# A memory layer on one NeuronCore: recall turned and values weighed as 32-row tiles, one per batch and head

## The reference, cut to what matters

```python
def step(carry, inp):                       # per batch b and head h, 32 tokens
    mem, z = carry                          # 64 x 64 and 64
    q_s, k_s, v_s, qn_s, kn_s = inp
    scores = einsum('bhnd,bhmd->bhnm', q_s, k_s) * SCALE      # rotated q, k
    sdpa = einsum('bhnm,bhmd->bhnd', softmax(where(mask, scores, -inf)), v_s)
    sq = elu1(qn_s)
    num = einsum('bhnk,bhkv->bhnv', sq, mem)
    den = einsum('bhnk,bhk->bhn', sq, z)[..., None]
    out = beta * num / (den + 1e-06) + (1.0 - beta) * sdpa
    sk = elu1(kn_s)
    prev_v = einsum('bhnk,bhkv->bhnv', sk, mem) / einsum('bhnk,bhk->bhn', sk, z)[..., None]
    mem = mem + einsum('bhnk,bhnv->bhkv', sk, v_s - prev_v)
    z = z + sk.sum(axis=2)
    return ((mem, z), out)
```

## Time and profile before

| | |
|---|---|
| median of 3 runs | 2612.66 us (2610.97 to 2617.28) |
| span of the profiled execution | 2623.8 us; no other time of this execution is given |
| memory layer in it | about 1729 to 2452 us |
| rounds with scores | 128, from 1760.2 to 2434.1 |
| `spread` on GpSimd | 128 x 1273 ns, 162.9 us |
| `weigh`'s first part (L2104) on TensorE | 512 records, 79.2 us |
| `weigh`'s second part (L2107) on TensorE | 1024 records, 85.5 us |
| granted TensorE clock | 1.00 from 1780 to 2425 (2.4 GHz), 0.72 on average from 1750 to 1780, 0.80 from 2425 to 2450 |
| busy from 2000 to 2100 | TensorE 94.4, VectorE 91.3, ScalarE 71.7, GpSimd 72.0 of 100 us |

### The profile page before, as it was taken

The page is one execution under the profiler, slowest core; times in us unless marked ns, Lnnn a source line. Parts: engine busy times, 40 slices in busy tenths (PEclk is TensorE's granted clock), DMA queues, the critical chain, the costliest instruction groups (busy, mean ns, idle before and its releaser), DMA issues. The chain is left out here.

```text
span 2623.8 us, 79243 instructions
## 1 busy us (share of the span) xinstructions
PE 2176.9 (83%) x30448; PEld 1549.2 (59%) x30448; DVE 1700.0 (65%) x5819; ACT 1437.8 (55%) x3704; POOL 1106.7 (42%) x1076
## 2 busy tenths in 40 slices
PE   6499948589964889899999977948999999999696
PEld 3288845379862233333334336937778777787396
DVE  6722247642336778787878833358999989899522
ACT  5455544355552256455455555537777767776353
POOL 2066644146654120120200004547777777776164
PEclk7699979789986799998989888969999999999798
DMA  4011120011125121111111000121111111111013
GB/s 133 33 42 43 43 85 2 33 32 44 43 93 163 55 58 31 38 39 31 35 46 35 5 33 29 41 85 54 54 53 56 52 53 55 52 56 52 35 42 92
DMA packets 76025, 134.96 MB, mean 51 GB/s; under 512 B 17225, under 2 KB 32264, under 8 KB 73224
## 3 DMA queue, kind: packets, MB, share of 16 engines
q1 hardware_dynamic: 62080, 102.07, 12.6%
q0 software_dynamic: 13568, 27.81, 3.7%
q10 hardware_dynamic: 8, 0.00, 0.0%
HBM read 65.19 MB, written 32.79 MB: 37 GB/s over the span
## 5 line engine op out<-in xcount | busy, mean ns | idle before, releaser
L1544 ACT ACTIVATE ca_pt<-ca_ps 128x512 f32<-128x512 f32 (+3 forms) x768 | 341.1, 491 | 322.3 <-PE ca_ps L1649 137.2
L734 PE MATMUL ffn_ps<-ffn_xst,ffn_up_w 128*128 128x128 f32 x3392 | 420.8, 278 | 0.2 <-issue 0.2
L734 PEld LDWEIGHTS ffn_ps<-ffn_xst,ffn_up_w 128*128 128x128 f32 x3392 | 402.9, 195 | 1.2 <-issue 1.2
L857 DVE TENSOR_TENSOR ffn_hid<-ffn_sg,ffn_ps 128x512 f32<-128x512 f32 x212 | 145.8, 688 | 359.2 <-PE ffn_ps L734 110.9
L576 POOL DMA_INDIRECT ffn_xs<-ffn_x,ffn_token_at x212 | 205.2, 968 | 301.5 <-DVE ffn_token_at L840 165.5
L581 POOL DMA_INDIRECT ffn_y<-ffn_ys,ffn_result_at x212 | 208.8, 985 | 139.2 <-DVE ffn_ys L863 82.3
L1645 PE MATMUL ca_ps<-ca_stacks 75*128 75x512 bf16 (+3 forms) x768 | 245.2, 342 | 18.3 <-ACT ca_pt L1544 10.7
L1777 DVE TENSOR_REDUCE ca_m_far<-ca_ps 128x1 f32<-128x128 f32 (+5 forms) x384 | 236.7, 616 | 30.3 <-PE ca_ps L1623 27.9
L643 ACT ACTIVATE ffn_sg<-ffn_ps 128x512 f32<-128x512 f32 x212 | 125.7, 593 | 233.6 <-remote 182.3
L1623 PE MATMUL ca_ps<-ca_stacks 72*128 72x512 bf16 (+3 forms) x768 | 223.4, 356 | 34.1 <-DVE ca_m_near L1778 21.9
L1778 DVE CUSTOM_DVE_ANT_0 ca_spill<-ca_ps,ca_bias_q 128x256 f32<-128x256 f32 (+1 forms) x512 | 201.1, 397 | 10.9 <-PE ca_ps L1623 10.9
(11 more groups left out here) (340 smaller groups left out, 4742.0 us busy)
## 6 DMA issues: line engine op xcount, KB each, us to landing
im_mates<-im_t SPq DMA_DIRECT2D x256, 128.0 KB
ffn_got<-ffn_y SPq DMA_DIRECT2D x48, 256.0 KB, 5.8
ca_stacks<-scratch_q_piece SPq DMA_DIRECT2D x16, 576.0 KB
ca_stacks<-scratch_k_piece SPq DMA_DIRECT2D x48, 192.0 KB
ffn_x<-ffn_xn SPq DMA_DIRECT2D x32, 256.0 KB, 2.0
w_w<-in_L_ffn_experts_w_dram SPq DMA_DIRECT2D x2, 2048.0 KB, 12.0
ffn_xs<-ffn_x,ffn_token_at POOLq DMA_INDIRECT x212
ffn_y<-ffn_ys,ffn_result_at POOLq DMA_INDIRECT x212
```

Source lines behind the costliest of these rows:

```text
L734: last = nc.tensor.matmul(ps[:, bank, j * P:j * P + P], up_w[:, n % WS, first + j * P:first + j * P + P], xst[:, n % 2, :], start=True, st ...
L1544: nc.scalar.activation(pt[:, i % 8, lo - c0:hi - c0], ps[:, tile_bank(i), lo - c0:hi - c0], ACT.Exp, scale=SCALE).then_inc(p_ready, 1)
```

## The change

`weigh` now uses 32 matmuls per piece: for each head and batch, one turns the 32 rows of `m1` against the 32x32 corner of the identity, and one weighs the 32 rows of v by the 32x32 block of `pt_g`. Each writes 64 rows by 32 columns. The four batches go to four banks, 4 to 7, at columns 192 to 255; the `w_out` products move to columns 256 to 511 of banks 6 and 7. `spread` becomes `gate_p`, the product of P transposed with the gate's share, without the block diagonal; `own`, its fills and `own_g` go, and four small copies that sort the share come. Since output and `w_out` products now share banks, `weigh` waits for the adds due by its round, `product` waits for the newest copy, and VectorE's `add` moves from behind `turn_p` to right behind `remember`.

```diff
-    UP, OT = 4, 192
+    UP, OT, OUT = 4, 192, 256
...
-        b_ot = ps[:, UP:UP + PB, OT:OT + P]
-        b_out = ps[:, UP + 2:UP + 4, OT:OT + 2 * P].rearrange("p c (d f) -> p c d f", f=P)
+        b_ot = ps[:, UP:UP + BATCH, OT:OT + PB * SEG]
+        b_out = ps[:, UP + 2:UP + 4, OUT:OUT + 2 * P].rearrange("p c (d f) -> p c d f", f=P)
...
-                nc.gpsimd.memset(own[:], 0.0).then_inc(S["made"], 1)
-                for b in range(BATCH):
-                    pool.wait_ge(S["made"], 9 + b)
-                    nc.gpsimd.memset(own[SEG * b:SEG * b + SEG, b, :], 1.0).then_inc(S["made"], 1)
-                pool.wait_ge(S["made"], 13)
...
                 for q in range(NQ):
-                    for e in range(2):
-                        shape = [P, PB, BATCH, SEG]
-                        gated = nc.gpsimd.tensor_tensor(own_g[:, q, e * PB:e * PB + PB], own[:].unsqueeze(1).to_broadcast(shape),
-                                                        share[:, q * QH + e:q * QH + QH:2].unsqueeze(2).unsqueeze(3).to_broadcast(shape), ALU.mult)
+                    gated = nc.gpsimd.tensor_copy(sorted_share[:, q].rearrange("p (e k) -> p k e", e=2), share[:, q * QH:q * QH + QH].rearrange("p (k e) -> p k e", e=2))
...
-                    shape = [P, QH, BATCH, SEG]
-                    nc.gpsimd.tensor_tensor(pt_e[:, j % 2], pt[:].unsqueeze(2).to_broadcast(shape), own_g[:, j % NQ], ALU.mult).then_inc(S["pte_ready"], 1)
+                    nc.gpsimd.tensor_tensor(pt_g[:, j % 2], pt[:], bl(sorted_share[:, j % NQ], SEG), ALU.mult).then_inc(S["ptg_ready"], 1)
...
-                    nc.scalar.activation(oT[:, w // 4 % 2, q * PB:q * PB + PB, :, w % 4, :], b_ot.rearrange("p n (b t) -> p n b t", t=SEG), ACT.Copy).then_inc(S["ot_copied"], 1)
+                    nc.scalar.activation(oT[:, w // 4 % 2, q * PB:q * PB + PB, :, w % 4, :], b_ot.rearrange("p b (n t) -> p n b t", t=SEG), ACT.Copy).then_inc(S["ot_copied"], 1)
...
-                    pe.wait_ge(S["pte_ready"], j + 1)
+                    if adds_by[j + 4]:
+                        pe.wait_ge(S["x_ready"], adds_by[j + 4])
+                    pe.wait_ge(S["ptg_ready"], j + 1)
                     for n in range(PB):
-                        nc.tensor.matmul(ps[:, UP + n, OT:OT + P], m1[:, j % 2, 2 * n:2 * n + 2, :].rearrange("p h d -> p (h d)"), g.ident[:], start=True, stop=False, skip_group_check=True)
-                    for n in range(PB):
-                        for e in range(2):
-                            last = nc.tensor.matmul(ps[D * e:D * e + D, UP + n, OT:OT + P], values_of(j)[:, 2 * n + e, :], pt_e[:, j % 2, PB * e + n].rearrange("p b t -> p (b t)"),
-                                                    start=False, stop=True, skip_group_check=True)
+                        heads = [(b, e, slice(SEG * b, SEG * b + SEG), ps[D * e:D * e + D, UP + b, OT + SEG * n:OT + SEG * n + SEG]) for b in range(BATCH) for e in range(2)]
+                        for b, e, tok, out in heads:
+                            nc.tensor.matmul(out, m1[tok, j % 2, 2 * n + e, :], g.ident[tok, tok], start=True, stop=False, skip_group_check=True)
+                        for b, e, tok, out in heads:
+                            last = nc.tensor.matmul(out, values_of(j)[tok, 2 * n + e, :], pt_g[tok, j % 2, PB * e + n, :], start=False, stop=True, skip_group_check=True)
...
-                    pe.wait_ge(S["ot_copied"], GROUP * i + 3 * NQ + first // PB + 1)
+                    pe.wait_ge(S["ot_copied"], min(k - 3, N))
...
                     if 0 <= k - 4 < LEARNED:
                         remember(k - 4)
+                    if k in added_in:
+                        add(added_in[k])
                     if k < N:
                         sines(k)
...
-                    if k in added_in:
-                        add(added_in[k])
```

More of the change, by code:

```diff
@@ L1885, in memory_layer @@
         pe_, pn, pt = s.sb("pe_", [P, QH, SEG]), s.sb("pn", [P, QH, SEG]), s.sb("pt", [P, QH, SEG])
-        pt_e = s.sb("pt_e", [P, 2, QH, BATCH, SEG])
-        own, share, own_g = s.sb("own", [P, BATCH, SEG]), s.sb("share", [P, H]), s.sb("own_g", [P, NQ, QH, BATCH, SEG])
+        pt_g = s.sb("pt_g", [P, 2, QH, SEG])
+        share, sorted_share = s.sb("share", [P, H]), s.sb("sorted_share", [P, NQ, QH])
         nm, sm, rs = s.sb("nm", [P, QH]), s.sb("sm", [P, 2, QH]), s.sb("rs", [P, QH])
@@ L1894, in memory_layer @@
         b_up = ps[:, UP:UP + BATCH, 0:PB * E1]
-        b_ot = ps[:, UP:UP + PB, OT:OT + P]
-        b_out = ps[:, UP + 2:UP + 4, OT:OT + 2 * P].rearrange("p c (d f) -> p c d f", f=P)
+        b_ot = ps[:, UP:UP + BATCH, OT:OT + PB * SEG]
+        b_out = ps[:, UP + 2:UP + 4, OUT:OUT + 2 * P].rearrange("p c (d f) -> p c d f", f=P)
         names = ("rows_loaded", "gate_loaded", "loaded", "made", "g_ready", "setup", "xn_ready", "turned", "xt_ready", "proj_ready", "t2_ready", "mates_even", "mates_odd",
                  "ab_used", "below_ready", "er_ready", "below_exp", "el_ready", "rope_ready", "lift_ready", "lifted", "scored", "recalled", "s1_ready", "rd_ready", "nm_ready",
-                 "u_ready", "den_ready", "dn_ready", "m1_ready", "p_ready", "share_ready", "own_gated", "rsum_ready", "pn_ready", "pt_ready", "pte_ready",
+                 "u_ready", "den_ready", "dn_ready", "m1_ready", "p_ready", "share_ready", "share_sorted", "rsum_ready", "pn_ready", "pt_ready", "ptg_ready",
                  "upd_ready", "mem_ready", "weighed", "ot_copied", "out_ready", "x_ready", "stats")
@@ L1977, in _, with gate_p @@
                 pool.wait_ge(S["made"], 8)
-                nc.gpsimd.memset(own[:], 0.0).then_inc(S["made"], 1)
-                for b in range(BATCH):
-                    pool.wait_ge(S["made"], 9 + b)
-                    nc.gpsimd.memset(own[SEG * b:SEG * b + SEG, b, :], 1.0).then_inc(S["made"], 1)
-                pool.wait_ge(S["made"], 13)
                 pool.wait_ge(S["share_ready"], 1)
                 for q in range(NQ):
-                    for e in range(2):
-                        shape = [P, PB, BATCH, SEG]
-                        gated = nc.gpsimd.tensor_tensor(own_g[:, q, e * PB:e * PB + PB], own[:].unsqueeze(1).to_broadcast(shape),
-                                                        share[:, q * QH + e:q * QH + QH:2].unsqueeze(2).unsqueeze(3).to_broadcast(shape), ALU.mult)
-                gated.then_inc(S["own_gated"], 1)
-                pool.wait_ge(S["own_gated"], 1)
-                def spread(j):
+                    gated = nc.gpsimd.tensor_copy(sorted_share[:, q].rearrange("p (e k) -> p k e", e=2), share[:, q * QH:q * QH + QH].rearrange("p (k e) -> p k e", e=2))
+                gated.then_inc(S["share_sorted"], 1)
+                pool.wait_ge(S["share_sorted"], 1)
+                def gate_p(j):
                     pool.wait_ge(S["pt_ready"], j + 1)
@@ L2018, in _ @@
                     if 0 <= k - 3 < N:
-                        spread(k - 3)
+                        gate_p(k - 3)
                     if k < N:
@@ L2176, in lift_keys @@
                     last.then_inc(S["lift_ready"], 1)
-                pe.wait_ge(S["made"], 13)
+                pe.wait_ge(S["made"], 8)
                 for c in range(2 * BATCH):
@@ L2217, in _ @@
                 dve.wait_ge(S["g_ready"], 1)
-                dve.wait_ge(S["made"], 13)
+                dve.wait_ge(S["made"], 8)
                 nc.vector.tensor_scalar_add(gate[:, 1:3, :], gate[:, 1:3, :], 1.0).then_inc(S["setup"], 1)
@@ L2252, in turn_p @@
                     if j:
-                        dve.wait_ge(S["pte_ready"], j)
+                        dve.wait_ge(S["ptg_ready"], j)
                     nc.vector.transpose(pt[:].rearrange("p a b -> p (a b)"), pn[:].rearrange("p a b -> p (a b)")).then_inc(S["pt_ready"], 1)
```

## The result

The changed kernel takes 2772.59 us (median of 4 runs, 2766.42 to 2784.13) against 2614.97 for the kernel before on the same chip (4 runs, 2610.97 to 2620.19): a ratio of 1.0608, with a 95% interval of 1.0580 to 1.0637. I had forecast 2582 and a range up to 2607; it went the other way, by 158 us.

What follows compares the result with a forecast made beforehand. It took a ring of waits, scores to weighing to `num` to VectorE's `m1` to scores, 5.11 us a round, as the bound. Rounds 24, start 4.5 and end 2.3 made 31 us off 2612.66: 2582, range 2560 to 2607.

Steps and rivals of the forecast that it cites:

- TensorE's own round: TensorE's own work in one round: 4.98 us before, 4.55 after the change, below the forecast round of 4.74.
- The new stage: Recall and weighing on TensorE as 32 small matmuls: 0.70 us in place of 1.13, saving 0.43 a round.
- What is late next: Softmax chain on ScalarE and VectorE bounds the round once 0.32 us is saved: plain rounds of 4.74 us.
- The add's wait: `weigh` waits for VectorE's moved output add: up to 0.1 or 0.2 us in such a round, costing nothing.
- GpSimd's product: Product of the gated P, 128x512 made 128x128: 1.27 us becomes 0.29 to 0.58, worth 0 in a round.
- The start: Start of the memory layer, without the fills of `own` and the `own_g` products: 4.5 us saved.
- The end: Four weighings after the last projection, where the other engines are empty: 2.3 us saved.
- Rival 1: The transfers rule, two thirds of rounds following them: 2594 us, or 2600 if adds pass on delay; chance 0.18.
- Rival 2: Stage as cheap as twice the scores, transfers keeping pace: 58 us gained with the ends, 2555 us; chance 0.08.
- Rival 3: The 64 records of the weighing take the old 1.13 us, only the start gains: 2608 us; chance 0.06.
- the ring: Cycle of waits from scores through weighing, `num` and VectorE's `m1` to the next scores: 5.11 us a round.
- Rival 4: Matmuls on the same TensorE rows can't overlap: stage 1.96 us, round 5.94, kernel 2706 us; chance 0.10.

Runs made afterwards that it cites:

- 26 pads: The kernel before with 26 more one-column f32 matmuls in every round, ahead of `num`: 2757.72 us, ratio 1.0586.
- turned pairs: The changed kernel with `m1` turned for two heads at once, 32x128 weights, 16 records fewer a round: 2657.80 us, ratio 1.0396.
- `num` first: The kernel before with `num` put ahead of the projection of v and of `weigh`, no instruction added: 2637.23 us, ratio 1.0102.
- burst: The kernel before with 1280 one-column f32 matmuls, without waits, ahead of the layer's first transposes: 2696.45 us (before 2622.10), one run.

## Why the prediction was wrong, point by point

**The step that failed** is in the part on the weighing: "TensorE's own round, 4.98 - 0.43 = 4.55, fits below." It counted what TensorE executes and not what it has to be given. 312 instructions a round became 416, and TensorE's own round went from 4.80 to 6.40 by supply while it fell by array time. With this one term left out, a gain of 24 us in the rounds was forecast, and they lost 146. Of its evidence the page of before had the record counts, the 250 packets of the instruction queue, and 4 stops for "issue" in `prev`; what a block costs stood in no row, because nothing in that kernel ran into it for long. An instruction count beside the time count, and the question what the four stops were, would have named it as a rival.

- **The new stage**: 0.70 forecast, 0.79 measured where nothing stopped it, against 1.13. Right in kind: the gain is 0.34, not 0.43.
- **What is late next**: forecast was the softmax, with rounds of 4.74. Only 17 rounds held no stop; their median was 5.35, and three were under 4.90. The softmax limit was not reached and is not tested.
- **The add's wait**: forecast nothing. `weigh` waited 6.0 us for it in 16 rounds; beside the stops that is little in the rounds, but see the end.
- **GpSimd's product**: 0.40, inside the bounds, and worth nothing in a round, as said.
- **The start**: 4.5 forecast, 4.6 measured. The recorded 1.2 us for the fills is 1.35 by its own rows (1733.15 to 1734.50), and the transposes came 1.0 sooner. Moving `own_g` alone, in the last experiment, brought nothing.
- **The end**: forecast 2.3 us saved; it lost 8.5. I had cost the two new waits by the rounds and not by the last weighings, where no other work lies between them: two of them waited 0.98 us each for the adds, and two products 0.47 and 0.48 for the copies. With those gaps and the stops TensorE fell to its lower clock level (0.57 over the stretch), and the last four products, 16 records each, take 3.78, 3.79, 3.78 and 3.75 us, where before they took 2.79, 2.05, 2.05 and 2.02. That is 6.2 us, and the waits are 2.9: 9.1 of the 10.8 us between forecast and result. Undoing these waits alone was not tried.
- **Rival 1**, transfers: more rotations waited (117 for 57), but without any transfers the round is the same. Not the cause.
- **Rival 2**, a stage as cheap as twice the scores (0.42): excluded by the 0.79.
- **Rival 3**, no gain in the ring: the ring did get shorter, and the time lengthened by another way.
- **Rival 4**, slower by row groups, had the right side and a round of 5.94, but that was luck, since its mechanism was wrong: the stage is 0.79 in either order. The Trainium skill ("TensorE: Matmul & The Clock Gate", The mechanism), whose rule spoke for it, is not borne out by this pair: the order that changes rows with every matmul and the one that keeps them for two both took 0.79 us.

The changed kernel's slowness is thus explained by the supply. Shown: that the time follows the instructions and not the array's time (26 pads, turned pairs), that every stop ends just behind the landing of a block, that row order in the stage and transfers play no part, and that a stream without waits comes in blocks of 256. Open: why the supply is not smooth below its limit. "`num` first" took a block per 4.51 us by its mean, and 3.94 was possible, yet 51 rounds ran dry. The stages of small matmuls lie together, and 256 of the smallest are gone in 1.34 us, so that the blocks may be asked for too late, as the 2.4 us to the next packet suggest; no run varied that.

## What to carry to other kernels

Cutting a matmul into small tiles is priced in instructions as well as in array time: count matmul records a round on TensorE, double them for the weight loads, divide by 256, and multiply by about 3.9 us, the figure of these kernels; where that comes near the round, a gain on the array is doubtful (`num` first), and past it the kernels here took that time whatever the array did. In a trace the sign is idle time with the releaser "issue" in the middle of a loop, evenly spaced and moving from stage to stage, with a packet of the instruction queue landing 1.1 to 1.8 us before each stop ends. The cure is fewer records: bf16 operands where the accuracy allows (one record in place of two) or wider tiles, even ones that take longer on the array.

## What the runs showed of the hardware that was not expected

- TensorE's instructions are fetched while the kernel runs: 250 packets of 16 KB before and 302 after. The Trainium skill ("Trainium Architecture — The Big Picture", The software stack) says that instructions have 64 bytes, and the trace agrees (0.85 MB over 13,312); that section has the streams brought into each engine's memory when the kernel is loaded and tells of no fetch after that, where this trace has one block after another within the execution.
- One block per 3.93 to 4.01 us in the rounds of the supply-bound kernels, 3.71 in the bare stream; 3.93 without the SP transfers.
- One-column matmuls with 64x32 weights on tiles side by side start every 9.1 ns in "burst" (128 starts within 1.155 us, the last over at 1.34) at a granted clock of 0.5. The Trainium skill ("TensorE: Matmul & The Clock Gate", Wait — 56ns, not 53.3ns?) puts the least distance of two starts at about 25 ns; for matmuls on different tiles the measurement decides.
- 32x128 weights on 32 columns took 0.35 for 8 records (2030.39 to 2030.74), 44 ns each, where 32x64 weights took 0.79/64 = 12 ns.
